# Drawing the next chunk's pieces two per head before heads 0 to 3, in place of one per head before heads 0 to 7

## The reference, cut to what matters

```
qkv = x @ w_qkv.T + b_qkv
zn   = z / max(|z|, 1e-12)              # z is q or k of a head
proj = zn @ omega                       # 2 nodes x 32 features
f    = proj**2/sqrt(32) * exp(clip(proj*sqrt(2s) - s, -20, 20)) / sqrt(32) * sqrt(w)
kv_cum = cumsum(kf x v);  k_cum = cumsum(kf)
ctx  = (qf . kv_cum) / max(qf . k_cum, 1e-6)
out  = ctx @ w_out.T + b_out
```

## Time and profile before

| | us |
|---|---|
| runs of the kernel, two | 4213.95 and 4362.6, median 4288.27 |
| the profiled execution, slowest core | 4208.98 |
| its span | 4207.4 |
| spans of the eight cores | 4160.7 to 4207.4 |
| PE, DVE, ACT busy | 2212.1, 902.5, 943.3 |

### The profile page before, as it was taken

How to read it: one execution, slowest core, us unless ns; L and a number is a source line. 1 busy time by engine, 2 the same in 40 slices (tenths; PEclk the granted TensorE clock), 3 DMA queues, 4 the chain that set the end, 5 groups by cost and what they waited for, 6 DMA issues and landing times.

```text
span 4207.4 us, 30287 instructions; the slowest of 8 cores (4160.7 to 4207.4 us)
## 1 busy us (share of the span) xinstructions
PE 2212.1 (53%) x10253; PEld 1002.5 (24%) x10368; DVE 902.5 (21%) x1526; ACT 943.3 (22%) x1313; POOL 51.5 (1%) x73
## 2 busy tenths in 40 slices
PE   0344334435445354353545666676663766666664
PEld 0222222223223132232221222222221222222222
DVE  0222222233323333332343000000004100000003
ACT  0222322323232322323102111111101311111111
POOL 1000000000000000000000000000000000000000
PEclk9666666657666566665556788887886888888887
DMA  8000000000000000000002221112223022222221
GB/s 169 5 6 11 5 5 5 1 0 1 0 0 1 0 1 1 1 0 1 1 7 40 40 40 29 27 25 40 40 40 80 1 40 40 40 40 40 40 40 40
DMA packets 55077, 99.55 MB, mean 24 GB/s; under 512 B 2368, under 2 KB 18880, under 8 KB 53824
## 3 DMA queue, kind: packets, MB, share of 16 engines
q0 software_dynamic: 44880, 80.82, 11.7%
q1 hardware_dynamic: 10048, 16.79, 1.2%
HBM read 170.03 MB, written 8.39 MB: 42 GB/s over the span
## 4 chain that ended last, share of the span: by engine, by line
PE 48%; DVE 19%; ACT 12%; DMA 11%; issue 7%; DVEq 2%; ACTq 1%; POOL 0%; SPq 0%; POOLq 0%
PE psB L803 24%; DMA wc<-wcT 8%; PE psA L396 6%; PE psA L766 4%; DVE oacc L821 3%; PE psA L429 3%; DMA xa_bf<-x_carry 2%; ACT qk_bf L406 2%; DVE railsM L528 2%; PE psB L601 1%; DVE pn_bf L346 1%; DVE f32s L319 1%; PE psA L272 1%; PE psA L339 1%; ACT f32s L323 1%
## 5 line engine op out<-in xcount | busy, mean ns | idle before, releaser
L803 PE MATMUL psB<-hsl,wc 128*128 128x512 bf16 x4004 | 1054.7, 407 | 550.3 <-DMA wc<-wcT 423.2
L803 PEld LDWEIGHTS psB<-hsl,wc 128*128 128x128 bf16 x4096 | 377.6, 102 | 1092.6 <-issue 771.7
L777 ACT ACTIVATE hsl<-psA 128x512 bf16<-128x512 f32 x512 | 305.7, 597 | 1351.3 <-PE psA L766 1347.1
L821 DVE TENSOR_TENSOR oacc<-oacc,psB 128x2048 f32<-128x2048 f32 x56 | 128.1, 2288 | 1441.8 <-PE psB L803 1441.8
L396 PE MATMUL psA<-ln_bf,wqkv_bf 128*128 128x256 bf16 x1536 | 233.1, 325 | 86.9 <-DVEq L83 56.3
L266 PE MATMUL psA<-xa_bf,allones_bf 128*128 128x256 bf16 x256 | 58.0, 404 | 372.5 <-DMA xa_bf<-x_carry 211.8
L766 PE MATMUL psA<-ln,railsM 32*128 32x512 bf16 x512 | 210.9, 414 | 24.5 <-DVEq L83 13.8
L396 PEld LDWEIGHTS psA<-ln_bf,wqkv_bf 128*128 128x128 bf16 x1536 | 175.0, 116 | 141.8 <-issue 95.1
L339 PE MATMUL psA<-qk_bf,omega_bf 64*64 64x256 bf16 x384 | 50.9, 413 | 212.0 <-DVEq L83 212.0
L262 ACT ACTIVATE sq_bf<-xa_bf 128x2048 bf16<-128x2048 bf16 x32 | 61.1, 1909 | 446.1 <-DVEq L83 284.0
L579 ACT ACTIVATE f32sB<-f32sB 64x256 f32<-64x256 f32 x128 | 53.0, 414 | 481.5 <-DVEq L83 481.5
(11 more groups left out here) (150 smaller groups left out, 2033.0 us busy)
## 6 DMA issues: line engine op xcount, KB each, us to landing
wc<-wcT POOLq DMA_DIRECT2D x32, 2048.0 KB, 18.0
x_sb<-x_own SPq DMA_DIRECT2D x8, 1024.0 KB, 23.4
y_out<-oacc SPq DMA_DIRECT2D x8, 1024.0 KB, 4.4
wqkv_bf<-wqkvT POOLq DMA_DIRECT2D x8, 768.0 KB, 48.1
xa_bf<-x_carry POOLq DMA_DIRECT2D x8, 512.0 KB, 5.9
wout_bf<-woutT POOLq DMA_DIRECT2D x8, 256.0 KB, 66.6
rut_bf<-rut POOLq DMA_DIRECT2D x4, 128.0 KB, 5.5
omega_bf<-omega POOLq DMA_DIRECT2D x2, 128.0 KB, 15.4
```

Source lines behind the costliest of these rows:

```text
L777: A_((lambda a, fcl=fcl, zsl=zsl, hb=hb: a.activation(hb[:, fcl * 512:(fcl + 1) * 512], psA[:, zsl * 512:(zsl + 1) * 512], AF.Gelu)), wait ...
L803: t.matmul(psB[:, ob * 512:(ob + 1) * 512], wcbufs[fcl // 8][:, (fcl % 8) * 1024 + obi * 128: (fcl % 8) * 1024 + (obi + 1) * 128], hb[:, f ...
L821: V_((lambda v, g=g, obg=obg: v.tensor_tensor(AP(oacc, obg * 4096 + g * 512, [[8 * 1024, 128], [1024, 4], [1, 512]]), AP(oacc, obg * 4096 ...
```

## The change

`pump` is called twice before each of heads 0 to 3, where it was called once before each of heads 0 to 7. There are eight calls in the head loop in both cases, and the three calls after it stay where they are, so the same pieces are appended in the loop; only their places among the heads differ.

```diff
             for hh in range(H):
-                if hh < 8:
+                if hh < 4:
+                    pump()
                     pump()
                 sl = hh % 2
                 base = sl * 1024
```

## The result

The changed kernel takes 1.0063 times as long as the kernel before, 95% interval 1.0045 to 1.0081; its median over 30 runs is 4252.4 us, that of the kernel before over 29 runs 4227.3 us. That is about +27 us (19 to 34), within 2%. The forecast was 4246 us, +37 us on a profiled execution of 4209.0 us. A few executions of either kernel are some per cent longer, with a lower clock on all cores of a die, and are left out of the ratio; the 4288.27 us that stood ahead of the prediction are the mean of one ordinary run and one such.

What follows compares the result with a forecast made beforehand. Main chunks were taken as bound by waits between engines, none full. Terms sum to +3.85 us by order and +1.5 by clock, +5.3 per chunk, +37 over seven: 4246 us from 4209.0; range 4218 to 4290.

Steps and rivals of the forecast that it cites:

- 1, four more bare heads: Stage B heads without a stage A piece beside them: twelve instead of eight, 5.15 us each, +20.6 us per chunk.
- 2, h0 before P2: Layer norm no longer waits on DVE for the first head; its Square follows L496 directly, -5.8 us per chunk.
- 3, h2 out of the gap of P3 and P4: Third head leaves the psA wait between the two q passes, where it was free: 0 by the order.
- 3, clock of P4: Second q pass loses PE clock behind a 2.58 us idle gap: +1.5 us per chunk, bounds 0 and +3.65.
- 4, h4 from between P5 and P6: First k pass no longer waits for the fifth head behind the q features: 27.4 to 18.2 us, -9.2 per chunk.
- 5, P6 to P7: Between the two k passes, the third head's matmuls follow the q features' tail: 7.8 to 8.4 us, +0.6 per chunk.
- 6, P7 to P8's Square: k features' Square no longer waits for the seventh head after the second k pass: 8.5 to 6.2 us, -2.35.
- P7 keeps its 3.65 us: Second k pass keeps its duration since PE idles only about 1 us before it; bounds 0 and +3.65, took 0.
- Nothing behind absorbs it: After the chunks, the FFN waits for attn_done_dv, so the whole +37 us reaches the end.
- A: Rival: loss nearly cancelled, second q pass and later matmuls keep the higher clock; +2 per chunk, 4223 us; chance 0.15.
- B: Rival: clock low in all four q and k passes, 4317 us; chance 0.05 beyond 2%, 0.12 for its milder half.
- C: Rival: faster, twelve bare heads at the higher clock save 7.8 us; -4 per chunk, 4181 us; chance 0.03.

Runs made afterwards that it cites:

- P1 with P2: Kernel before, with only the x copy and layer norm drawn together before the first head; chunk period 177.81 us against 177.67.
- P5 with P6: Kernel before, with only the q features and first k pass drawn together before one head; chunk period 175.56 us against 177.67.
- P7 with P8: Kernel before, with only the second k pass and k features drawn together before one head; chunk period 180.94 us against 177.67.
- The changed order and the order before, both with overlapped heads: Both schedules, with each bare head's next scores and mask appended right behind this head's max; chunk periods 159.97 us (changed) and 162.66 us (before).
- the kernel with P3 and P4 together: Kernel before, with only the two q passes drawn together before one head; chunk period 184.16 us against 177.67.
- four pieces at a time: Kernel before, with four stage A pieces drawn before each of the first two heads, fourteen bare heads; chunk period 194.91 us against 177.67.

## Why the prediction was right or wrong

Against the traces, in us per chunk; the second chunk is the one that the prediction read:

| step | predicted | second chunk | mean of seven |
|---|---|---|---|
| 1, four more bare heads | +20.6 | +20.7 | +20.6 |
| 2, h0 before P2 | -5.8 | -5.8 | -5.5 (-3.5 in the first) |
| 3, h2 out of the gap of P3 and P4 | 0 | 0 | 0 |
| 3, clock of P4 | +1.5 | 0 | 0 |
| 4, h4 from between P5 and P6 | -9.2 | -9.15 | -9.0 |
| 5, P6 to P7 | +0.6 | +0.4 | +0.65 |
| 6, P7 to P8's Square | -2.35 | -2.3 | -1.65 |
| clock of P3 | 0 | +0.8 | +0.4 |
| layer norm to P3, and end of h15 to the next L496 | 0 | -0.9 | -0.4 |
| sum | +5.3 | +3.7 | +5.2 |

**Direction and order.** The steps that come from the order of the queues hold within 0.2 us each in the second chunk of the changed kernel. The kernels with one pair show the same: L262 5.8 us earlier behind L496 (P1 with P2), 18.2 us from Square to P6 (P5 with P6), 6.16 us from P7 to P8's Square (P7 with P8). The changed order and the order before, both with overlapped heads, confirm the reason: four bare heads at 5.15 us cost more than the joined pieces give back, and at 3.22 us they cost less.

**Step 3, the clock of P4,** is the term that was mis-sized. I took 5.12 us from stage A alone, where P3 takes 5.96 us behind a wait of 6.07. In the changed kernel P3 is over in 4.7 to 5.5 us and P4 keeps 3.65 us through the same gap. So the idle gap alone, by which the term was priced, does not lose the clock. That a head ahead of P3 is what saves P4 is not shown: the kernel with P3 and P4 together has h1 there, and its P4 loses the clock in five of seven chunks. Seven times 1.5 us were too much.

**Step 5, "P7 keeps its 3.65 us"**, holds in four chunks and fails in three, where P7 takes 5.2 to 5.3 us. It named +3.65 as the other bound and took 0. The prediction has 14.6 us from P6 to P8's Square; the three chunks take 16.8 to 17.0, the others 14.3 to 14.4, so over the seven it comes to 5 to 6 us more than priced. P3, slower by 0.4 us in the mean, adds 2.7; the first chunk, where L262 waits for L381 on ACT and not for L496, adds 2.3. Together these make up for the missing 10 us of step 3. That the sum came out within 1 us of the attention's +36.3 is so in part by luck: two of the prediction's own signs of being wrong (P4 at 3.65 us; P6 and P7 losing the clock) both came, and they pull opposite ways.

**"Nothing behind absorbs it"** is the step by which the forecast missed the measured ratio: +0.9% was forecast, +0.63% (0.45 to 0.81) measured. That the FFN waits for the attention is so, but it was put down as the whole answer with no row for it: the attention does take 36 us more, about 10 of them don't arrive at the end, and why is open. The forecast of 4246 us also stood on an execution of 4209 us, while the kernel before has its median at 4227: the absolute time came out right, 6 us under the measured median, because a base 18 us low and a difference 10 us high partly cancel. Against the 4288.27 us that stood ahead of it, 4246 us would even read as a gain; the prediction set that median aside for the profiled execution, and 4227.3 us over 29 runs bears that out, though 4209 was still too low.

**The rivals.** Of A, P4's clock came true, and h2's matmuls behind P6 run at the higher level in the second chunk (DVE waits 1.41 us for them at 1042.67), which step 5 had priced already; P8's run at 0.50 there (1054 to 1060 us). It forecast +2 per chunk, and +5.2 came. B, the clock low in all four passes, comes nearest with four pieces at a time (194.9 us, where the order alone gives 189.5), though no pass reaches B's 7.3 us; the changed kernel has it in two passes of three chunks. C needed bare heads at the higher clock; they are at 5.16 us.

## What to carry to other kernels

When pieces of one stage are spread between the steps of another, price each place by the wait that it covers: here one pair of neighbours gave back 9.2 us and another nothing, under one rule of the loop. A head that stood in a gap where its neighbours waited anyway was free there and cost its whole chain elsewhere. Where the bare chain is what a schedule loses to, shorten the chain first: taking the next mask ahead of the end of this head gave 4%, the best choice of places that was tried 0.3%.

## What the runs showed of the hardware

The duration of a pass of 32 matmuls depends on more than what stands right ahead of it: the same instructions behind the same waits take 5.0 and 3.67 us in one chunk and 6.4 and 5.3 us in another, with the granted clock at 0.71 and 1.00 or 0.56 and 0.69, and the pattern is the same on all eight cores and in two executions. Across an idle gap of 2.58 us the clock stayed at full in all chunks of the changed kernel (P4 3.65 us, behind a P3 of 4.7 to 5.5) and was lost in five of seven of the kernel with P3 and P4 together (P4 5.1 us, behind a P3 of 5.8 to 6.0). So the clock's part of a change does not add up over its edits (+7.8 us in four edits, +5.2 in all), while that of the order does (+3.9 both times).
